# A wavelet kernel's second pass: stores and loads on one queue, four and four in turn in place of two and two

## The reference

```python
yl, yh = _dwt2(x, _LEVEL)
yl_out = jnp.einsum('bixy,ioxy->boxy', yl, w_yl)
yh_out = yh[:-1] + [jnp.einsum('bicxy,iocxy->bocxy', yh[-1], w_yh)]
return _idwt2(yl_out, yh_out)
```

## Time and profile before

| What | us |
|---|---|
| median of 3 runs (lowest, highest) | 2045.24 (2045.2, 2045.88) |
| the profiled execution, its own time | 2047.34 |
| span of the profiled execution | 2045.2 |
| first pass, about | 0 to 660 |
| mixing, about | 660 to 778 |
| second pass, about | 778 to 2045 |

### The profile page before, as it was taken

The page is one execution under the profiler, slowest core; times in us unless marked ns, Lnnn a source line. Parts: engine busy times, 40 slices in busy tenths (PEclk is TensorE's granted clock), DMA queues, the critical chain, the costliest instruction groups (busy, mean ns, idle before and its releaser), DMA issues.

```text
span 2045.2 us, 44244 instructions
## 1 busy us (share of the span) xinstructions
PE 1853.3 (91%) x17580; PEld 945.5 (46%) x17580; DVE 837.0 (41%) x947; ACT 460.4 (23%) x1043; POOL 3.6 (0%) x7
## 2 busy tenths in 40 slices
PE   6999999999999679999998898898899889889886
PEld 3656666666666444444343333343333333334332
DVE  1222222222222454555444444444444444444443
ACT  1223222222322452121121121121121121112110
POOL 0000000000000000000000000000000000000000
PEclk9999999999999799999999999999999999999998
DMA  9999999999999695999999999999999999999998
GB/s 401 385 374 415 421 422 422 421 422 422 422 421 419 251 334 213 375 418 427 427 427 427 427 426 427 427 427 427 426 423 415 421 414 420 413 415 421 416 419 347
DMA packets 114794, 827.16 MB, mean 404 GB/s; under 512 B 12752, under 2 KB 13520, under 8 KB 17488
## 3 DMA queue, kind: packets, MB, share of 16 engines
q1 hardware_dynamic: 114768, 826.78, 97.7%
HBM read 558.29 MB, written 268.44 MB: 404 GB/s over the span
## 4 chain that ended last, share of the span: by engine, by line
DMA 52%; PE 10%; SPq 3%; issue 2%; DVE 0%; ACT 0%; DVEq 0%
DMA out<-x_sb 49%; PE ps L486 6%; DMA both<-w_full 2%; PE ps L476 2%; SPq L277 1%; PE ps L442 1%; SPq L282 1%; DMA x_sb<-x 1%; PE ps L437 1%; DMA both<-w_rest 0%; PE ps L466 0%; SPq L276 0%; DVE x_sb L720 0%; ACT both L610 0%; ACT both L570 0%
## 5 line engine op out<-in xcount | busy, mean ns | idle before, releaser
L486 PE MATMUL ps<-spread,const 128*128 128x512 f32 x2048 | 932.8, 598 | 109.5 <-DVE x_sb L720 109.5
L720 DVE TENSOR_TENSOR x_sb<-ps,x_sb 128x1024 f32<-128x1024 f32 x500 | 602.3, 1223 | 632.0 <-DMA x_sb<-x 403.0
L486 PEld LDWEIGHTS ps<-spread,const 128*128 128x128 f32 x2048 | 381.2, 190 | 645.2 <-issue 455.7
L624 ACT COPY spread<-ps 84x512 f32<-84x512 f32 x256 | 149.0, 582 | 938.5 <-PE ps L476 938.2
L350 PE MATMUL ps<-x_sb,const 32*32 32x512 f32 x8192 | 290.2, 601 | 36.6 <-DMA x_sb<-x 31.8
L363 PEld LDWEIGHTS ps<-const,work 128*128 128x128 f32 x2048 | 248.4, 194 | 56.4 <-ACT work L524 41.9
L476 PE MATMUL ps<-const,pick 128*84 128x512 f32 x512 | 261.3, 592 | 0.7 <-issue 0.7
L363 PE MATMUL ps<-const,work 128*128 128x84 f32 x2048 | 257.2, 278 | 2.9 <-ACT work L524 2.9
L524 ACT COPY work<-ps 128x512 f32<-128x512 f32 x256 | 131.4, 599 | 414.4 <-PE ps L350 414.4
L669 DVE COPY work<-ps 128x336 f32<-128x336 f32 x256 | 130.1, 508 | 176.3 <-PE ps L363 176.3
L350 PEld LDWEIGHTS ps<-x_sb,const 32*32 32x32 f32 x8192 | 138.3, 103 | 138.1 <-issue 98.7
(11 more groups left out here) (22 smaller groups left out, 218.9 us busy)
## 6 DMA issues: line engine op xcount, KB each, us to landing
x_sb<-x SPq DMA_DIRECT2D x498, 1024.0 KB, 13.3
out<-x_sb SPq DMA_DIRECT2D x250, 1024.0 KB, 16.8
both<-w_full SPq DMA_DIRECT2D x30, 896.0 KB, 6.6
work<-x SPq DMA_DIRECT2D x6, 1024.0 KB, 9.2
out<-work SPq DMA_DIRECT2D x6, 1024.0 KB, 10.8
both<-w_rest SPq DMA_DIRECT2D x6, 224.0 KB, 3.2
const<-consts SPq DMA_DIRECT2D x1, 888.0 KB, 4.5
```

The source lines that it names most:

```text
L486: last = nc.tensor.matmul(ps[:, 2 + k], const[:, SH + P * k:SH + P * k + P], spread[:, p], start=True, stop=True)
L624: nc.scalar.copy(spread[0:ROWS, p], ps[0:ROWS, p]).then_inc(s_copied[p], 1)
L720: nc.vector.tensor_tensor(part, ps[:, 2 + 2 * half:4 + 2 * half], part, ALU.add).then_inc(added[half], 1)
```

## The change

Only SyncE's program for the second pass changes. `BURST` is 4: four stores and then four loads are issued in turn. The loads are again those of the group of slots stored one group before: after the stores of slots 4 to 7 come the loads of slots 0 to 3, and after the stores of slots 0 to 3 those of slots 4 to 7. No transfer is added or left out, the waits in front of each store and each load are the same, and the other engines' programs are as before. `turn(2)` is written out ahead of the loop, since slots 4 and 5 have their images of turn 2 by then.

```diff
+BURST = 4
...
-            for c in range(0, SLOTS, 2):
-                store(c, 0, IMAGES - SLOTS)
-                store(c + 1, 0, IMAGES - SLOTS)
-                after_first(c)
-                after_first(c + 1)
...
+            def reload(c, t):
+
+                refill(c, t, IMAGES - SLOTS - SLOTS * t)
+
+            for c in range(0, SLOTS, BURST):
+                for d in range(c, c + BURST):
+                    store(d, 0, IMAGES - SLOTS)
+                for d in range(c - BURST, c):
+                    if d >= 0:
+                        reload(d, 2 if d < EARLY else 1)
...
-            with sp.Fori(2, TURNS - 1) as t:
...
-                for c in range(0, SLOTS, 2):
-                    store(c, t, first)
-                    store(c + 1, t, first)
-                    for d in (c, c + 1):
-                        if d < 2:
-                            refill(d + SLOTS - 2, t, first)
-                        else:
-                            refill(d - 2, t + 1, after)
...
+            def turn(t, loaded=()):
                 first = t * -SLOTS + (IMAGES - SLOTS)
                 after = t * -SLOTS + (IMAGES - 2 * SLOTS)
...
+                for c in range(0, SLOTS, BURST):
+                    for d in range(c, c + BURST):
+                        store(d, t, first)
+                    for d in range(c - BURST, c):
+                        if d >= 0:
+                            refill(d, t + 1, after)
+                        elif d + SLOTS not in loaded:
+                            refill(d + SLOTS, t, first)
+
+            turn(2, loaded=range(BURST, EARLY))
+            with sp.Fori(3, TURNS - 1) as t:
+                turn(t)
```

More of the change, by code:

```diff
@@ L307, in _ @@
                         store(d, 1, IMAGES - 2 * SLOTS)
-                after_second(c)
-                after_second(c + 1)
-            with sp.Fori(2, TURNS - 1) as t:
+                for d in range(c - BURST, c):
+                    if d < 0:
+                        reload(d + SLOTS, 2 if d + SLOTS < EARLY else 1)
+                    elif d >= EARLY:
+                        reload(d, 2)
+            def turn(t, loaded=()):
                 first = t * -SLOTS + (IMAGES - SLOTS)
                 after = t * -SLOTS + (IMAGES - 2 * SLOTS)
-                for c in range(0, SLOTS, 2):
-                    store(c, t, first)
-                    store(c + 1, t, first)
-                    for d in (c, c + 1):
-                        if d < 2:
-                            refill(d + SLOTS - 2, t, first)
-                        else:
-                            refill(d - 2, t + 1, after)
[L321 to L326, removed]
+                for c in range(0, SLOTS, BURST):
+                    for d in range(c, c + BURST):
+                        store(d, t, first)
+                    for d in range(c - BURST, c):
+                        if d >= 0:
[5 more added lines that the diff above has]
+                turn(t)
+            for c in range(0, SLOTS, BURST):
+                for d in range(c, c + BURST):
+                    store(d, TURNS - 1, 0)
+                for d in range(c - BURST, c):
+                    if d < 0:
+                        refill(d + SLOTS, TURNS - 1, 0)
             sp.wait_ge(early_stored, 16 * EARLY)
```

## The result

| | before | changed |
|---|---|---|
| median of 4 runs, us (lowest, highest) | 2045.43 (2045.2, 2045.88) | 2311.8 (2304.66, 2316.73) |
| ratio to the kernel before | | 1.129 (1.126 to 1.132) |
| profiled execution, its own time | 2047.34 | 2312.07 |
| span | 2045.2 | 2310.0 |
| DMA queue, share of 16 engines | 97.7% | 90.2% |

The change costs 266 us. 2259 were forecast, with a range of 2158 to 2322; the measured time lies 10 us inside its upper end.

The account below looks back on a forecast made before the run. The second pass was taken as bound by TensorE, then by the DMA engines. Image 23 ends at 887.9 us; 58 rounds of 23.34 (1353.7), 12.2 for batches and 5.2 at the end give 2259 us, range 2158 to 2322.

Parts of the forecast that it names:

- The mechanism: Second pass: loads wait behind the fourth store and its add, so compute and load of successive groups no longer overlap.
- The ring: Second pass, images 24 to 255: compute and load of groups of four in series, 58 rounds.
- The size of a round: Four images in the second pass: 14.84 + 6.9 + 1.6 = 23.34 us, against 19.9 before.
- the batches: Coefficient preparation on TensorE, in images 2 and 3 of a group: 0.87 us each, 12.2 us in all.
- the clock: TensorE's pause of 4.3 us each round brings the half clock: 1.6 us a round, granted clock about 0.93.
- part two: Each round, from the fourth store's issue to the landing of the load behind it: 6.9 us, between 6.4 and 7.4.
- The forecast of the DMA share: Second pass, 940 to 2000 us: share falls to 0.85, rate to about 359 GB/s.
- Rival (a): The clock holds through TensorE's pauses, or falls within them only: 2166 us, chance 0.15.
- The start: Second pass before image 24: late first loads make image 15 end 3.4 us late, and this stays.
- The end: After the last add, the last store lands sooner in an empty queue: 5.2 us in place of 9.6.
- (b): Rival: each pause of TensorE costs 3.0 us or more by a longer half clock: 2340 us, chance 0.09.
- (c): Rival: a load runs beside a store at full rate and lands after 4.4 us: 2021 us, chance 0.04.

Follow-up runs that it names:

- e1: Changed kernel with the loads one store earlier in the cycle, behind the stores of slots 2 and 6: 2110.5 us, 1.031 of the kernel before.
- e5: Changed kernel with the loads two stores earlier in the cycle, behind the stores of slots 1 and 5: 2059.4 us, 1.0087 of the kernel before.
- e7: Changed kernel with two extra products (1.72 us) on TensorE ahead of each group's third image, except in batch-preparing turns: 2436.7 us.
- e8: Kernel before, in pairs, with the same extra 1.72 us of products ahead of every fourth image: 2052.3 us, ratio 1.003.
- e3: Changed kernel with four unread products (3.4 us) filling TensorE's pause in most groups: 2239.2 us, 1.093 of the kernel before.
- e2: Changed kernel with the four loads issued ahead of the fourth store, behind the same add: 2207.2 us, 1.079 of the kernel before.
- e6: Changed kernel with BURST = 1, one store and one load in turn: 2117.7 us, 1.036 of the kernel before.
- e11: One store and one load in turn, loading the slot stored two before instead of one: 2105.4 us, 1.027 of the kernel before.

## Why the prediction was right, and what was off

**The mechanism held, each step where it was put.** SyncE's 212 waits for landed stores (940 to 2000 us) are gone, and it waits at the stores, for adds. The ring began at image 24 and made 58 rounds, all visible as 58 waits of VectorE. e1 and e5 opened it by moving the loads alone; e7 against e8 showed that compute is in series with the transfers in the changed order and beside them in pairs.

**The size of a round was off.** The last add of image 23 ended at 891.9 (its store and the loads behind it follow at once, 892.28 in the rows above) and the last add of all at 2305.6, so a round took 24.4 us: 14.82 from the start of the first add to the end of the fourth at full clock (as e3's filled rounds have it), 7.59 from there to the next group's first add, 0.2 for the batches and some 1.77 for the clock. I had 23.34 and the 0.2 beside it. Of the 53 us that the forecast fell short, 48 are 58 times the 0.83 missing in each round, of which some 0.67 lie in part two and 0.17 in the clock. The range held because its upper end was set with 7.4 us for part two and 2.2 for the clock.

**The term that was mis-sized is part two**, 6.9 us between ends of 6.4 and 7.4. It measured 7.59 as VectorE's wait. In the two rounds of the chain above it is 7.51 and 7.59. Of this, 0.17 and 0.03 lie between the add's end and the store (1502.67 to 1502.84 with SyncE's register work in between, 1526.69 to 1526.72 without), and 0.11 between landing and add (1510.06 to 1510.17). I had counted 0.02 and nothing. The rest, store's issue to landed load, was 7.2 (1502.84 to 1510.06) and 7.4 us (1526.72 to 1534.17) in two rounds. This is the high end, the one measured with a load behind the store; the low end was built from a store that had nothing behind it. The changed kernel shows both, from issue to landing: the stores at 1518.1 and 1522.4, and then the fourth store at 1526.7 with its load behind it:

```profile
DMA to landing us min/median/max: 3.9/4.5/5.1
...
DMA to landing us min/median/max: 5.0/5.0/5.0
```

The 3.9 are the store at 1522.4, with nothing behind it and the one before it landing 0.8 us after its issue. The 5.1 are the store at 1518.1, which had an earlier store still ahead of it and says nothing here. The middle between two rows was the wrong choice, as one of them had the same neighbours as the case and the other had not. The queue's rate over 1500 to 1530, 0.75 us a slice, shows where the 1.1 us go:

```profile
GB/s 426 98 0 0 120 404 360 339 175 295 437 415 448 382 481 393 459 393 437 437 328 284 251 415 426 448 382 481 371 404 22 502 371 426 98 0 175 371 437 251
```

The fourth store's data run from slice 5 on; in slices 9 and 10 (1506.0 to 1507.5), where the store ends and the load begins, the rate is 175 and 295. It is 328, 284 and 251 again in slices 21 to 23 (1515.0 to 1517.25), where the last load ends and the first stores begin. Between the two lie 7.5 us of loads at 428 on average. The zeros ahead of slice 5 are the empty queue that the prediction asked for. The forecast of the DMA share missed in the same place: 0.88 at 344 GB/s from 940 to 2000, where 0.85 at 359 were forecast. The rate fell further than the share, so a byte kept the engines busy longer than in pairs.

**The clock.** Forecast 1.6 us a round and 0.93; some 1.77 and 0.92 were seen, behind pauses of 4.9 us on average where 4.3 were forecast. The image behind the pause took 5.13 to 6.66 us in all 58 rounds, 5.46 on average, where e3 has 3.70. By the Trainium skill (TensorE: Matmul & The Clock Gate, the section on HAM oscillation), a loop that waits for a DMA each turn restarts cold each turn; the trace agrees, with 5.40 and 5.94 us for the image behind two pauses in a row and a clock of 0.92 throughout. Rival (a), 2166 us without the fall, is out; e3 shows what it would be worth. That these pauses lay far beyond 1.99 us was what the step needed: shorter ones were not always followed by a fall (last section).

**The start.** 6.6 us late, not 3.4. Of the 3.2 between them, 1.4 are the clock, which the sum left out at this place:

```profile
849.90 2.36 DVE L721 TENSOR_TENSOR x_sb<-ps,x_sb 128x1024 f32<-128x1024 f32 x2 [7.60 <-DMA x_sb<-x]
851.18 5.10 PE L487 MATMUL ps<-spread,const 128*128 128x512 f32 x8 [4.99 <-DVE x_sb L721]
```

TensorE paused for 4.99 us ahead of image 15, and from VectorE's start on image 14 to the end of image 15 it took 7.65 us in place of 6.24. The other 1.9 are the load of image 14, which landed later than the 12 transfers of 2.49 us would have it. Why they took longer I have not separated. One slip without effect: image 19's store was put at 871.5, and by the same sum it is 870.7.

**The end.** 4.4 us from the last add to the end of the span (2305.6 to 2310.0), where 5.2 were forecast and 9.6 had been.

**The rivals.** (b), longer falls of 3.0 us or more, is out for the changed kernel, whose falls cost some 1.77. (c), a load beside a store, is out: the load behind a store took 6.6 us at the least from its issue.

## What to carry to other kernels

Where one engine issues loads and stores in order, ask of each load which add or product stands ahead of it in that order. If the load of the next group waits for the last result of this one, compute and transfer form a ring whose length is the sum of both; the remedy is to issue the loads some stores earlier, and here one store earlier gave back three quarters of the loss and two nearly all, with the groups unchanged. When a latency in such a ring is priced, take the row whose neighbours in the queue are the same, and add the fall of TensorE's clock where the pause is as long as those behind which it always fell, here from about 4 us on; between 2 and 3.7 us it fell behind about half.

## What the runs showed of the hardware

- **The clock after a pause.** With `out_stage` on TensorE an image behind a pause takes 3.70 us at full clock. It took that behind all 18 pauses of 1.3 to 1.95 us in e1, e2 and e5 (from 880 us on). Behind every pause of 3.76 us or more, in these runs and in the changed kernel, it took 5.13 us or longer. Between 2 and 3.7 us both were seen: in 39 of the 77 such pauses of the three runs the clock stayed full, and in the other 38 it fell. In e1 a pause of 3.69 us was followed by the full clock and one of 2.15 by the half; in e5, in the rows below, 2.54 by the full and 2.52 by the half. So the length of the pause alone does not decide, and what does is not shown. The 1.99 us of the kernel before and the 1.55 in its first pass are no threshold.
- **Time is lost where a store and a load meet in a queue that has just been empty.** A store followed by a load lands about 1.1 us later than one followed by nothing, and the rate dips at both changes of direction and not from load to load. Whether a second store behind the first would delay it as much was not tried. It is not a cost of four and four as such: e5 makes the same changes at 416 to 420 GB/s. In the kernel before, with two and two, the mixed queue ran at 427, above the first pass's reads alone (413). How deep the queue stays goes with the rate: stores landed after 5.0 us (median) at 344 GB/s in the changed kernel, 9.4 at 397 in e6, 9.7 at 402 in e1, 13.9 at 416 to 420 in e5, 17.6 at 417 to 427 in pairs. e11, 14.4 us and yet 373 GB/s in its second stretch, does not fit, and its cause is open.

Two rows of e5, on the first point:

```profile
1330.65 3.70 PE L478 MATMUL ps<-spread,const 128*128 128x512 f32 x8 [2.54 <-DVE x_sb L712]
...
1350.60 5.23 PE L478 MATMUL ps<-spread,const 128*128 128x512 f32 x8 [2.52 <-DVE x_sb L712]
```
